# Spreading first in each slot, and one bank for the rows of both norms, in a convolution-attention and mixture-of-experts block

## The chip, the cores and the metric

One core of one Trainium2 chip. The metric is the device time of one execution in microseconds (us); the kernel before takes 705.34 us, the median of three runs (703.17 to 705.60).

## The reference

For x of shape (4, 64, 128, 128), fp32, per pixel (token) of 64 channels:

```python
n = ln_c(x)                                  # over channels, eps 1e-6
k, q, v = relu(Wk n + bk), relu(Wq n + bq), Wv n + bv      # 8 heads of 8 channels
context = einsum('bhkn,bhvn->bhkv', k, v)    # one sum over all 16384 pixels of an image
x = x + Wr einsum('bhkv,bhkn->bhvn', context, q) + br
t = tokens(x); m = ln_t(t)                   # over channels, eps 1e-5
p = softmax(m @ router_w + router_b)         # 8 experts, the two largest kept, scaled to sum 1
x = t + sum_over_two(p_e * (m @ expert_w[e] + expert_b[e]))
```

## The kernel before

The pixels are cut into 32 groups of 2048 (`GROUPS`, 8 for each image); a group is two halves of the image rows on partitions 0 to 63 and 64 to 127 (`S` = 2), in two halves of 512 columns (`U` = 2). The program is one long software pipeline of 49 steps (`STEPS`) of four slots each, and every engine walks through the same loop over steps `n` and slots `k`, written by hand. A stage with lag `L` works at step `n` on group `n - L`. In a step with all stages at work TensorE does, in order:

- slot 0: `make_keys` (L936, L943), `to_columns` twice (transposing the row statistics of both norms, L1006), `turn_x` (L911);
- slot 1: `sum_up` (the context's sums, L974), `turn_back` (L921);
- slot 2: `attend` (L1020), `make_queries` (L960);
- slot 3: `turn_gates` (L1045), `measure_x` and `route` (both through `rows_of`, L986: for each token the mean, the mean square and the router's products).

Each slot then ends with two pieces of the expert stage. `broadcast(i)` (the spreading, L1059) copies the gate of a pair of experts to 64 partitions per expert for the two iterations of the next slot; from its banks VectorE multiplies one half with x (`product`, L816, writes `z`) and ScalarE copies the other (`copy_gates`, L571, writes `gbs`) for GpSimd to multiply (L431). `experts(i)` (L1073, L1076, opened once per half group by the bias product L1070) multiplies `z` of this slot's two iterations with the expert weights, in an output bank of its own. There are 8 iterations per group, 2 per slot (`PER_SLOT`). `experts` with j = 0 waits until VectorE's `result` (L826) has taken the output bank of the half group before; `result` stands in slots 0 and 2.

All other products go through six banks in turn. `bank_uses` lists the uses in the program's order; a use waits until the use six places before it was taken out of its bank:

```python
USE = {use: (i % ROUND, i // ROUND + 1) for i, use in enumerate(bank_uses())}
```

VectorE's queue holds in each slot: fold, `result`, `add_sums` (L688), `x_deviations` (a chain of 7 small operations, L654 to L657 and L642 to L644), `residual` (L720), a piece of `gates` (27 operations for two groups, spread over 8 slots by `gates_by_phase`, with a square root and an exponential on ScalarE between them), `normalise` (L676), and last the two products of the slot. GpSimd does its products first in each slot and the squares of x (L422) in slot 1. ScalarE takes the other banks.

## Time and profile before

| | |
|---|---|
| median of 3 runs | 705.34 us |
| profiled execution | 708.03 us, its span 706.2 us |
| TensorE busy | 647.4 us, 92% |
| VectorE busy | 532.2 us, 75% |
| ScalarE busy | 428.5 us, 61% |
| GpSimd busy | 396.5 us, 56% |
| mean granted TensorE clock | 0.99 |

PE is TensorE, PEld its weight loads, DVE VectorE, ACT ScalarE, POOL GpSimd, SP the engine that issues most transfers. Busy times are unions over an engine's instructions, so the shares are averages over stretches of the pipeline in which different stages work: from step 0 to 16 no experts, from step 32 on no more loading of x. In a timeline a line is one instruction or a run of like ones; the ends of matmuls are modelled and overlap the next start, so distances are read from start to start. A matmul of fp32 shows as two passes.

### The profile page before, as it was taken

To read this page: it belongs to the slowest core of one execution; us is meant where nothing else is said; L and a number is where in the kernel's file an instruction comes from. 1 tells how busy PE (TensorE), PEld (TensorE's weight loads), DVE (VectorE), ACT (ScalarE), POOL (GpSimd) and SP (SyncE) were. 2 spreads that over 40 slices of the span, in tenths; PEclk is the share of its full clock that TensorE was granted. 3 is DMA by queue.
4 is the path that set the end of the run, shared out by engine and by line. 5 is a ranking of instruction groups with operands and counts; after the bars stand their busy time and mean duration, and the time that the engine had idled before them with its cause. 6 is when DMAs were issued, how large, how long until landed. Compare 5 with 4: busy or idle time off the path is not lost.

```text
span 706.2 us, 20616 instructions
## 1 busy us (share of the span) xinstructions
PE 647.4 (92%) x7846; PEld 302.0 (43%) x7846; DVE 532.2 (75%) x1176; ACT 428.5 (61%) x852; POOL 396.5 (56%) x350
## 2 busy tenths in 40 slices
PE   3898999799999999999999999999989889896786
PEld 1676766444544444444544444444322223231221
DVE  3443456878788988888788988867889998978853
ACT  2354556857566676657576776756656666564542
POOL 7132342165456566565456566555657667575785
PEclk9999999999999999999999999999999999999999
DMA  6232544655565555555566564444656555454442
GB/s 141 61 75 71 130 122 122 169 145 123 136 151 135 136 140 125 127 136 123 133 150 148 123 148 99 98 111 107 149 130 152 120 120 135 102 131 97 107 104 46
DMA packets 32660, 86.16 MB, mean 122 GB/s; under 512 B 7650, under 2 KB 7826, under 8 KB 32562
## 3 DMA queue, kind: packets, MB, share of 16 engines
q1 hardware_dynamic: 32082, 84.64, 50.7%
q8 instruction: 63, 1.03, 0.7%
q0 software_dynamic: 288, 0.19, 0.1%
q14 instruction: 35, 0.29, 0.1%
q10 hardware_dynamic: 192, 0.01, 0.0%
HBM read 34.47 MB, written 16.78 MB: 73 GB/s over the span
## 4 chain that ended last, share of the span: by engine, by line
PE 68%; DVE 13%; ACT 10%; issue 7%; DMA 1%; POOL 1%; DVEq 0%; SPq 0%; ACTq 0%; POOLq 0%
PE bank L1073 25%; PE bank L1059 8%; PE bank L986 5%; PE bank L921 5%; PE bank L974 5%; PE bank L943 4%; PE bank L911 4%; ACT grows L565 3%; DVE z L816 3%; PE bank L1020 3%; PE bank L1006 2%; ACT L543 2%; DVE osb L826 2%; PE bank L1070 2%; DVE x L720 2%
## 5 line engine op out<-in xcount | busy, mean ns | idle before, releaser
L431 POOL TENSOR_TENSOR z<-gbs,x1d 128x512 f32<-128x512 f32 x256 | 320.6, 1275 | 220.7 <-ACT gbs L571 164.8
L1076 PE MATMUL bank<-z,ew 128*64 128x512 f32 x512 | 248.0, 607 | 0.0
L1073 PE MATMUL bank<-z,ew 128*64 128x512 f32 x512 | 247.9, 607 | 0.0
L571 ACT COPY gbs<-bank 128x512 f32<-128x512 f32 x256 | 140.0, 593 | 95.3 <-PE bank L1059 94.4
L816 DVE TENSOR_TENSOR z<-bank,x1d 128x512 f32<-128x512 f32 x256 | 162.9, 677 | 20.4 <-PE bank L1059 20.1
L1059 PE MATMUL bank<-grows,sel 64*64 64x512 f16 x1024 | 89.3, 388 | 28.2 <-DVE z L816 17.0
L422 POOL TENSOR_TENSOR xsq<-xin 128x512 f32<-128x512 f32 x64 | 65.6, 1046 | 81.8 <-DMA xin<-in_x_dram 78.2
L1073 PEld LDWEIGHTS bank<-z,ew 128*64 128x64 f32 x512 | 65.7, 138 | 105.6 <-issue 95.8
L492 ACT COPY xn<-bank 128x512 f32<-128x512 f32 x64 | 34.6, 588 | 68.2 <-PE bank L921 68.2
L676 DVE TENSOR_TENSOR xnT<-bank,rstd 128x512 f32<-128x512 f32 x64 | 41.3, 684 | 39.2 <-PE bank L911 37.0
L1059 PEld LDWEIGHTS bank<-grows,sel 64*64 64x64 f16 x1024 | 24.1, 104 | 97.2 <-issue 34.4
L1076 PEld LDWEIGHTS bank<-z,ew 128*64 128x64 f32 x512 | 65.6, 138 | 0.0
L826 DVE TENSOR_TENSOR osb<-bank,x 128x512 f32<-128x512 f32 x64 | 43.8, 685 | 23.1 <-PE bank L1076 23.1
L565 ACT COPY grows<-bank 128x1024 f16<-128x1024 f16 x32 | 32.3, 1010 | 30.3 <-PE bank L1045 30.3
L474 ACT ACTIVATE keys<-bank 128x512 f32<-128x512 f32 x64 | 34.8, 595 | 25.4 <-PE bank L943 25.4
L720 DVE SCALAR_TENSOR_TENSOR x<-bank,br_col,x_again 128x512 f32<-128x512 f32 x64 | 44.9, 743 | 5.2 <-PE bank L1020 4.8
L482 ACT ACTIVATE q<-bank,bq_col 128x512 f32<-128x512 f32 x64 | 40.6, 689 | 7.2 <-PE bank L960 7.2
L974 PEld LDWEIGHTS bank<-xnT,keys 128*64 128x64 f32 x1024 | 34.7, 139 | 13.3 <-issue 12.2
L974 PE MATMUL bank<-xnT,keys 128*64 128x66 f32 x1024 | 36.7, 225 | 1.2 <-ACT keys L474 1.0
L921 PE MATMUL bank<-k,xnT 128*128 128x128 f32 x256 | 35.9, 284 | 1.7 <-DVE xnT L676 1.2
L532 ACT ACTIVATE x1sq<-x 128x512 f32<-128x512 f32 x64 | 37.4, 645 | 0.0
L943 PEld LDWEIGHTS bank<-wk_bd,xn 64*64 64x64 f32 x2048 | 35.5, 135 | 4.2 <-issue 1.9
(138 smaller groups left out, 885.0 us busy)
## 6 DMA issues: line engine op xcount, KB each, us to landing
x1d<-x SPq DMA_DIRECT2D x128, 256.0 KB, 4.5
xin<-in_x_dram SPq DMA_DIRECT2D x64, 256.0 KB, 4.1
x_again<-in_x_dram SPq DMA_DIRECT2D x64, 256.0 KB, 4.1
out_dram<-osb SPq DMA_DIRECT2D x128, 128.0 KB, 2.4
k<-in_const_dram SPq DMA_DIRECT2D x1, 453.5 KB, 3.7
ew_nat<-in_L_ffn_expert_w_dram POOLq DMA_DIRECT2D x2, 64.0 KB, 6.5
sel<-in_const_sel_dram SPq DMA_DIRECT2D x1, 128.0 KB, 3.5
bk_rows<-bk_wide ACTq DMA_DIRECT2D x6, 1.0 KB, 1.7
```

What stands on the lines that cost most here:

```text
L422: pool.tensor_tensor(xsq[:, u * NT:(u + 1) * NT], half, half, ALU.mult).then_inc(x_squared, 1)
L431: pool.tensor_tensor(z[:, 1, i % R_Z, :], gbs[:, i % R_Z, :], x1d[:, g % 2, 1, u * NT:(u + 1) * NT], ALU.mult).then_inc(z_pool, 1)
L571: nc.scalar.copy(gbs[:, i % R_Z, :], bank[:, :]).then_inc(taken_of(("spread", i, 1)), 1)
L720: dve.scalar_tensor_tensor(x1[:, g % R_X1, half], bank[:, :], br_col[:, 0:1], x_again[:, g % 2, half], ALU.add, ALU.add).then_inc(taken_of ...
L816: dve.tensor_tensor(z[:, 0, i % R_Z, :], bank[:, :], x1d[:, g % 2, 0, u * NT:(u + 1) * NT], ALU.mult).then_inc(taken_of(("spread", i, 0)), 1)
L826: dve.tensor_tensor(osb[:, g % 2, half], out_bank[:, :], x1[:, g % R_X1, half], ALU.add).then_inc(out_done, 1)
L921: ins = pe.transpose(bank[:, j * P:(j + 1) * P], xnT[:, g % 2, u, j, 1:P + 1], eye)
L943: ins = pe.matmul(banks[s][C * a:C * a + C, j * C:(j + 1) * C], xn[rows, g % 2, j * P + C * a:j * P + C * a + C], wk_bd[rows, rows], start ...
L974: ins = pe.matmul(bank[C * s:C * s + C, 0:C + 2], keys[:, s, at:at + C], xnT[:, g % 2, u, j, C * s:C * s + C + 2], start=(u == 0 and j == ...
L1059: ins = pe.matmul(bank[cols, :], sel[rows, j, cols], grows[rows, g % 2, u * NT:(u + 1) * NT], start=True, stop=True)
L1073: pe.matmul(out_bank[0:C, :], ew[:, j, :], z[:, 0, i % R_Z, :], start=False, stop=(j == PAIRS - 1), skip_group_check=True).then_inc(prod_d ...
L1076: pe.matmul(out_bank[C:P, :], ew[:, j, :], z[:, 1, i % R_Z, :], start=False, stop=(j == PAIRS - 1), skip_group_check=True).then_inc(prod_d ...
```

## The change

Four edits:

1. In each slot of each engine's loop the expert stage's parts that concern the next slot come first: `broadcast` on TensorE, `product` on VectorE, `copy_gates` on ScalarE. `experts` stays last. `x_deviations` moves behind the gates on VectorE, `root_x` from slot 1 to slot 2, `square_x1` ahead of the rows' eviction on ScalarE.
2. The row statistics of the norm of x (group n) and of the router (group n - 12) are accumulated in one bank, at other rows of it (`NROW` = 24 of each 32), taken with one eviction to `rows_sb`, and turned by one pair of transpositions instead of two; ScalarE takes two slices of that one bank, `lg` and `xs`.
3. `turn_gates` and the eviction of the gate rows move from slot 3 with lag 16 to slot 1 with lag 17. The experts' lag goes from 17 to 18, so that there are 50 steps. The ring of x1 has 8 places instead of 7.
4. The pieces of the gates chain are cut and placed anew.

```diff
-L_COLS, L_TURN, L_KEYS, L_AGAIN, L_ATTEND, L_ROUTE, L_GATES, L_TURN_GATES, L_EXPERTS = 1, 2, 3, 9, 11, 12, 14, 16, 17
+L_COLS, L_TURN, L_KEYS, L_AGAIN, L_ATTEND, L_ROUTE, L_GATES, L_TURN_GATES, L_EXPERTS = 1, 2, 3, 9, 11, 12, 14, 17, 18
-R_X, R_Q, R_X1, R_Z = 3, 8, 7, 4
+R_X, R_Q, R_X1, R_Z = 3, 8, 8, 4
...
-            p, late = divmod(SLOTS * (n - L_GATES) + k - 1 - phase, 2 * SLOTS)
+            p, late = divmod(SLOTS * (n - L_GATES) + k - 3 - phase, 2 * SLOTS)
...
-            gate_steps = {0: root_dev, 5: exponent, 7: high, 8: low}
+            gate_steps = {0: root_dev, 4: exponent, 7: high, 8: low}
...
-            gates_by_phase = {8: (26, 27), 0: (0, 4), 2: (4, 9), 3: (9, 12), 4: (12, 16), 6: (16, 20), 7: (20, 26)}
+            gates_by_phase = {8: (26, 27), 0: (0, 4), 1: (4, 8), 2: (8, 13), 4: (13, 16), 5: (16, 18), 6: (18, 24), 7: (24, 26)}
...
+            def take_cols(n):
+
+                bank = when_filled(act, ("cols", n, 0))
+                columns = bank[:, 0:U * P].rearrange("p (a r) -> p a r", r=W)
+                g = n - L_ROUTE
+                if real(g):
+                    upto(act, gate_dve, (g // 2 - 2) * N_GATE + 8)
+                    half = g % 2 * U * NJ
+                    ins = nc.scalar.copy(lg[:, g // 2 % 2, half:half + U * NJ, :], columns[:, :, 0:NLG])
+                if real(n):
+                    upto(act, xstat_dve, n * N_XSTAT)
+                    ins = nc.scalar.copy(xs[:, :, :], columns[:, :, NLG:NROW])
+                ins.then_inc(taken_of(("cols", n, 0)), 1)
...
+            def make_rows(n):
...
+                for part, (tile, weights) in enumerate(parts):
+                    chunks = tile.rearrange("p (u j n) -> p u j n", u=U, j=NJ)
                     for j in range(NJ):
-                        ins = pe.matmul(outs[j], weights, chunks[:, :, j, :], start=start, stop=not start,
-                                        skip_group_check=True)
+                        out_rows = bank[W * j:W * (j + 1), 0:U * P].rearrange("p (u n) -> p u n", u=U)
+                        ins = pe.matmul(out_rows, weights, chunks[:, :, j, :], start=(part == 0),
+                                        stop=(part == len(parts) - 1), skip_group_check=True)
...
                 for k in range(SLOTS):
+                    for i in iterations(n, k + 1):
+                        product(i)
+
                     if folding(n, k):
                         fold(*folding(n, k))
                     if k == 0 and real(n - L_EXPERTS - 1):
                         result(n - L_EXPERTS - 1, 1)
...
-                    for i in iterations(n, k + 1):
-                        product(i)
...
                 for k in range(SLOTS):
+                    for i in iterations(n, k + 1):
+                        broadcast(i)
+
                     if folding(n, k):
                         fold(*folding(n, k))
...
-                    for i in iterations(n, k + 1):
-                        broadcast(i)
                     for i in iterations(n, k):
                         experts(i)
```

TensorE's queue in slots 1 and 2 of a full step, before (L974 context sums, L921 turning back, L1059 spreading, L1073 and L1076 experts, L1020 attention, L960 queries, L1070 bias product):

```order
257 L974 MATMUL bank<-xnT,keys 64x66 x16
258 L921 MATMUL bank<-k,xnT 128x128 x8
259 L1059 MATMUL bank<-grows,sel 64x512 x8
260 L1073 MATMUL bank<-z,ew 64x512
...
264 L1020 MATMUL bank<-q,att 64x512 x4
265 L960 MATMUL bank<-xn,wq 64x512 x4
266 L1059 MATMUL bank<-grows,sel 64x512 x8
267 L1070 MATMUL bank<-grows,eb_rows 64x512 x2
268 L1073 MATMUL bank<-z,ew 64x512
```

The same place in the changed kernel, whose line numbers differ (L1045 is now the spreading, L960 the context sums, L907 turning back, L1031 the gates' turning, L1006 attention, L946 queries, L1056 the bias product, L1059 an expert product):

```order
262 L1045 MATMUL bank<-grows,sel 64x512 x8
263 L960 MATMUL bank<-xnT,keys 64x66 x16
264 L907 MATMUL bank<-k,xnT 128x128 x8
265 L1031 MATMUL bank<-eye,gT 128x128 x8
266 L1059 MATMUL bank<-z,ew 64x512
...
270 L1045 MATMUL bank<-grows,sel 64x512 x8
271 L1006 MATMUL bank<-q,att 64x512 x4
272 L946 MATMUL bank<-xn,wq 64x512 x4
273 L1056 MATMUL bank<-grows,eb_rows 64x512 x2
274 L1059 MATMUL bank<-z,ew 64x512
```

The spreading now stands between the experts of the slot before and the slot's other work, and the bias product behind that other work. VectorE's queue at the start of slot 1 and in slot 2 of a step, before (L688 add_sums, L654 to L657 the first half of x_deviations, L762 to L788 gates, L816 the products, L826 `result`, L720 residual):

```order
335 L688 TENSOR_TENSOR s_acc<-bank,s_acc 128x66
336 L654 SCALAR_TENSOR_TENSOR xstat<-xs 128x16
...
339 L657 RECIPROCAL xstat<-xstat 128x16
340 L762 TENSOR_REDUCE gstat<-bank 128x32
...
343 L762 TENSOR_REDUCE gstat<-bank 128x32
344 L816 TENSOR_TENSOR z<-bank,x1d 128x512 x2
345 L826 TENSOR_TENSOR osb<-bank,x 128x512
346 L720 SCALAR_TENSOR_TENSOR x<-bank,br_col,x_again 128x512 x2
347 L816 TENSOR_TENSOR z<-bank,x1d 128x512 x2
```

and in the changed kernel (L803 the products, L675 add_sums, L770 to L749 gates, L641 to L644 x_deviations, L813 `result`, L707 residual):

```order
325 L803 TENSOR_TENSOR z<-bank,x1d 128x512 x2
326 L675 TENSOR_TENSOR s_acc<-bank,s_acc 128x66
327 L770 TENSOR_TENSOR bank<-bank,rb_row 128x256
...
331 L749 TENSOR_REDUCE gstat<-bank 128x32
332 L641 SCALAR_TENSOR_TENSOR xstat<-xs 128x16
...
335 L644 RECIPROCAL xstat<-xstat 128x16
336 L803 TENSOR_TENSOR z<-bank,x1d 128x512 x2
337 L813 TENSOR_TENSOR osb<-bank,x 128x512
338 L707 SCALAR_TENSOR_TENSOR x<-bank,br_col,x_again 128x512 x2
```

The products of a slot have moved from its end to its start, so that in slots 0 and 2 `result` stands behind products whose spreading is issued in the same slot.

## Rows read from the trace of the kernel before

**Rows 1.** Stretch, its us, busy PE PEld DVE ACT POOL, clock, DMA share, GB/s

```profile
0.00:143.41 143.41, 122.66 (x2226) 82.48 (x2226) 72.32 (x232) 76.55 (x173) 47.33 (x65) 0.99 0.47 113
143.41:440.38 296.97, 292.90 (x3674) 140.19 (x3674) 247.56 (x539) 197.96 (x398) 180.38 (x151) 1.00 0.56 133
440.38:497.32 56.94, 54.31 (x672) 24.89 (x670) 44.32 (x96) 38.36 (x73) 30.34 (x26) 1.00 0.48 115
497.32:634.25 136.93, 122.16 (x913) 38.06 (x913) 120.34 (x227) 83.80 (x155) 89.95 (x72) 0.98 0.54 126
634.25:706.20 71.95, 55.33 (x368) 16.39 (x366) 47.65 (x83) 31.85 (x56) 48.49 (x40) 0.97 0.40 92
```

**Rows 2.** Timeline, TensorE, a full step: start, us, line, [idle before <-releaser]

```profile
301.67 0.41 PE L936 MATMUL bank<-bk_rows,ones 64*64 64x512 bf16 x4
...
303.22 0.38 PE L1006 MATMUL bank<-k,route_rows 128*128 128x128 f32 x2
303.43 1.04 PE L911 MATMUL bank<-k,xin 128*128 128x128 f32 x8
304.40 0.63 PE L1059 MATMUL bank<-grows,sel 64*64 64x512 f16 x8
...
311.39 1.09 PE L1020 MATMUL bank<-q,att 64*64 64x512 f32 x8
...
313.16 0.60 PE L1059 MATMUL bank<-grows,sel 64*64 64x512 f16 x6
313.98 0.40 PE L1059 MATMUL bank<-grows,sel 64*64 64x512 f16 x2 [0.22 <-DVE x L720]
...
318.24 0.61 PE L986 MATMUL bank<-x1sq,k 128*32 128x256 f32 x8
318.95 0.63 PE L1059 MATMUL bank<-grows,sel 64*64 64x512 f16 x8
...
321.37 0.41 PE L936 MATMUL bank<-bk_rows,ones 64*64 64x512 bf16 x4
```

**Rows 3.** The same, TensorE, in step 47

```profile
684.86 0.63 PE L1059 MATMUL bank<-grows,sel 64*64 64x512 f16 x8
685.75 0.41 PE L1070 MATMUL bank<-grows,eb_rows 128*64 128x512 f16 x2 [0.26 <-DVE osb L826]
...
687.80 0.62 PE L1045 MATMUL bank<-eye,gT 128*128 128x128 f16 x8
689.53 0.63 PE L1059 MATMUL bank<-grows,sel 64*64 64x512 f16 x8 [1.10 <-ACT grows L565]
```

**Rows 4.** The same, VectorE, in step 47

```profile
685.00 0.69 DVE L826 TENSOR_TENSOR osb<-bank,x 128x512 f32<-128x512 f32 x1 [0.83 <-PE bank L1076]
...
690.03 1.29 DVE L816 TENSOR_TENSOR z<-bank,x1d 128x512 f32<-128x512 f32 x2 [3.14 <-PE bank L1059]
```

**Rows 5.** Groups by line: count, busy us, mean ns, idle before

```profile
L422 POOL TENSOR_TENSOR xsq<-xin 128x512 f32<-128x512 f32 x64 | 65.6, 1046 | 81.8 <-DMA xin<-in_x_dram 78.2 <-PE bank L986 3.6
...
L768 DVE TENSOR_TENSOR bank<-bank,gstat 128x256 f32<-128x256 f32 x32 | 13.8, 432 | 11.6 <-ACT gex L543 11.0
```

**Rows 6.** Timeline, GpSimd, step 47

```profile
690.73 4.97 POOL L431 TENSOR_TENSOR z<-gbs,x1d 128x512 f32<-128x512 f32 x4 [2.17 <-issue]
```

**Rows 7.** The same, GpSimd and VectorE, in step 36

```profile
516.75 2.50 POOL L431 TENSOR_TENSOR z<-gbs,x1d 128x512 f32<-128x512 f32 x2 [1.81 <-ACT gbs L571]
...
518.11 1.19 DVE L777 TENSOR_TENSOR bstat<-bstat,lg 128x32 f32<-128x32 f32 x1
```

**Rows 8.** The same, TensorE, keys' first product of steps 13, 16 and 17

```profile
102.38 0.41 PE L936 MATMUL bank<-bk_rows,ones 64*64 64x512 bf16 x4
...
128.12 0.41 PE L936 MATMUL bank<-bk_rows,ones 64*64 64x512 bf16 x4
...
143.41 0.41 PE L936 MATMUL bank<-bk_rows,ones 64*64 64x512 bf16 x4 [1.31 <-issue]
```

**Rows 9.** The same, TensorE, step 36

```profile
522.12 1.06 PE L1073 MATMUL bank<-z,ew 128*64 128x512 f32 x1
```

## What it does to the time: the prediction

> **What bounds the kernel now.** I read the busy table by stretches first, then TensorE's timeline in a full step, in the filling steps and in the tail, then what VectorE and GpSimd do beside it. The table by stretches [rows 1] is cut where the pipeline changes: filling (steps 0 to 16), full (17 to 31, 297.0 us), thinning (32 to 34), tail with gates, attention and experts (35 to 43, 136.9 us), and the last experts (44 to 48, 72.0 us). In the full stretch TensorE is busy 292.9 of 297.0 us: it is the bound, at 2.4 GHz, and VectorE follows with 247.6. In the tail TensorE has 122.2 of 136.9, in the last stretch 55.3 of 72.0; there waits decide.
>
> A full step takes 19.70 us (301.67 to 321.37) [rows 2]. Its TensorE waits are small: 0.22 us in slot 2, where the last spreading waits for a bank that VectorE's residual holds, and in slot 3 about 0.2 us, since the squares' products that started at 318.24 would be through by 318.75 and the spreading waits for the gate rows that ScalarE has just copied. The second transposition takes 0.21 us (303.22 to 303.43) [rows 2]. So what the change can win in a full step is: 0.2 transposition, 0.2 and 0.2 waits, one change of tile shape fewer (the first copy of an array shape takes 0.5 where a repeated one takes 0.4; I count 0.15 for the change), 0.25 for spreading beside keys and queries, which have its shape. Together 1.0: TensorE's own work becomes 18.7 us (slots of 5.06, 4.99, 4.36 and 4.28).
>
> **What the new order makes wait.** The bias product of a half group opens the output bank again, so it needs `result`, VectorE's eviction of the half before. Before, VectorE did `result` at once in slots 0 and 2. Now it does the two products of the slot first, and these need the spreading that TensorE issues at the slot's start. From the tail: spreading at 689.53, products from 690.03 when VectorE is idle (0.50; I take 0.47), the next instruction 1.20 after the first product's start (two take 1.29, ends overlap), `result` 0.69 [rows 3, 4], bias product 0.06 after it (osb from 685.00 + 0.69, bias 685.75) [rows 3, 4]. So the bias product can't start before 0.47 + 1.20 + 0.69 + 0.06 = 2.42 us into slots 0 and 2. Before it was 685.75 - 684.86 = 0.89 [rows 3]. What TensorE has in between hides it or not:
> - Slot 0 of a full step: spreading 0.48, then 304.40 - 301.67 - 0.21 = 2.52: 3.00 us [rows 2]. Hidden if VectorE is less than 0.6 late.
> - Slot 2: 0.48 + (313.16 - 311.39) + 0.1 = 2.33 us [rows 2]. No slack at all: any lateness of VectorE is TensorE idle time.
> - Slots 0 and 2 in the tail: 0.9 to 1.4 us, and at the end 0.56: 1.0 to 1.9 us of idle time each.
>
> **Is VectorE late in slot 2?** In slot 1 it now has two products (to 1.67), add_sums (to about 2.0), then five or six gate steps of 0.43 + 0.03 each (to 4.0 to 4.2) [rows 5] and the first four steps of x_deviations. GpSimd's products start 1.20 us after the spreading (690.73 against 689.53) and take 1.24 each [rows 3, 6]; with the two squares behind them at 1.02 each [rows 5] it is busy from 1.2 to 5.7 us of the slot. A small VectorE operation that starts beside one of GpSimd's takes as long as what is left of it: 1.19 us at 518.11 for 128x32 elements, ending at 519.30, 0.05 after GpSimd's second product (516.75 + 2.50) [rows 7]. Before, the four steps of x_deviations ran while GpSimd was idle; now two of them (in even steps a gate step too) fall beside its squares. I get VectorE free 6.3 us after slot 1's start, slot 2 starting at 5.0 and its products wanted at 5.5: 0.4 to 0.9 late, so 0.4 to 1.0 idle on TensorE in slot 2. In odd steps the square root and `low` on ScalarE stand ahead of slot 0's copies, the three Newton steps of the gates fall beside GpSimd's products, `normalise` ends at about 5.8 to 6.2 and sum_up waits up to 0.6 for its bank. Both kinds of step come to 18.7 + 0.95 = **19.65 us**: the win is given back.
> The Trainium skill (SBUF - State Buffer, Who interferes with whom) says that a VectorE instruction with two SBUF inputs, or in a two-port mode, shares a port pair with GpSimd as an exclusive lock. By that the held ones are the same as in the rows, so its sum is mine; it also lets VectorE hold GpSimd, for which the rows give no size.
>
> **The extra step.** Gate copies and turning move to slot 1 of a step later, so experts start in step 18 and there are 50 steps, not 49. Evictions of rows and columns on ScalarE (0.39 and less) lie beside other work; the x1 ring of 8 and the DMA queue's order change no wait that I see: the spread x1 of a group is still asked for more than a step ahead.
>
> **The sum**, in us of the profiled span:
> - Filling: steps 13 to 15 take 8.58 each (102.38 to 128.12) and step 16 takes 15.29, with VectorE's first gates in it [rows 8]. Those three lose 0.21 each. Steps 16 and 17 now share the gate work that crowded step 16: VectorE some 11 and 10.8, TensorE 8.4 and 9.5. 102.38 + 25.1 + 21.8 = 149.3; 143.4 before: +5.9.
> - Full: 14 x 19.65 + 1.5 (folding, 297.0 - 15 x 19.70) = 276.6: -20.4.
> - Thinning: the full step less the x rows (0.87), then also GpSimd's squares and less lateness, then also turning and back (2.0): 18.8 + 18.1 + 16.4 = 53.3: -3.6.
> - Tail, nine steps: slots 4.48 (2.42 + bias 0.24 + experts 1.82), 2.98, 4.48, 3.4 = 15.3, plus VectorE's lateness, 0.5 in slot 2 and 1.0 in every other slot 0: 16.4. 147.6: +10.7.
> - The last: three steps of 15.9 with gates left, two of 4.48 + 2.98 + 4.48 + 2.43 = 14.35, and 17.4 with the store (2.43 is the spreading's 0.56 + (687.80 - 685.75 - 0.24) + 0.05 [rows 3]): 93.8 against 72.0: +21.8. The 1.10 us that spreading waited for the gate rows goes here [rows 3], but 2 x 1.53 more wait for `result` come.
> - Clock: in the tail of before it was at 1.2 GHz for some stretches (an expert product takes 1.06 us at 522.12, where it takes 0.59 at full clock) [rows 9], 1.5 us each time, three times. TensorE was then idle for 1.5 us and shorter pieces. Idle stretches of 1.9 to 2.9 us twice a step are longer: as many drops or more; +3. The ends are no drop beyond those three, 0, and one more in each of ten steps, +15.
> Total 5.9 - 20.4 - 3.6 + 10.7 + 21.8 + 3 = +17.4. The profiled execution took 708.03 (span 706.2), the median is 705.34; taken from the median: 722.7, said as **722 us**.
>
> **Rivals.**
> - VectorE is not late (15%). The held operations fall into GpSimd's gaps, for instance since its products start later. Decides below 0.1 us of lateness in slot 2. Then the full step is 18.7 and the tail step 15.85: 149.3 + 263.3 + 52 + 142.7 + 91.1 = 698.4, -7.8: **697.5 us**, faster. For it: my slot schedule is made of 0.2 us pieces; against it: VectorE has 247.6 us of work in 297.0 already [rows 1], before more of it is held.
> - Only the tail pays (15%): full steps at 18.9, tail as forecast: 149.3 + 266.1 + 52 + 147.6 + 93.8 = 708.8, +2.6: **708 us**, about no change.
> - The clock halves in most tail steps (15%): ten drops of 1.5 more: **736 us**. For it: TensorE's share goes from 89% to about 83% in the tail and from 77% to about 60% at the end, and before the mean clock is 0.98 and 0.97 there against 1.00 in the full stretch [rows 1]. Against: 0.98 also says that most of the tail's waits cost no clock. The Trainium skill (TensorE: Matmul & The Clock Gate, HAM oscillation) has the clock fall to half where TensorE idles between bursts, and advises against such gaps; that rule speaks against this change and is this rival's mechanism.
> - The merging does less than it says: the order shows one pair of transpositions where two were, so only its size (0.2 a step, in 20 steps, 4 us) can be off; inside the range.
>
> **Chances.** Forecast 55%, the rivals 15% each. A difference under 0.5% (3.5 us) can't be told from no change. Faster: the first rival and a bit of the second, 17%; the same: 13%; slower: 70%. Range: 700 to 738; the first rival's centre and the worst of the clock are left out, together under 2 in 10.
>
> **What would show it.** Right: 50 steps, the first expert product near 152 us; full steps of 19.4 to 19.9 us with TensorE waiting 0.4 to 1 us ahead of the bias product in slot 2, released by `result`; in the last steps 4.4 to 4.5 us for slots 0 and 2 with 1.8 us of idle time there; no wait for the gate rows; mean of VectorE's small operations in slot 1 raised. Wrong: full steps at or below 18.9 us, or bias products released by anything else. Then the lateness of VectorE was mis-sized.

## The result and the profile after

The changed kernel takes **739.4 us** (median of four runs, 737.7 to 740.9) against 705.5 for the kernel before on the same chip: a ratio of 1.048, 95% interval 1.043 to 1.053. It is slower, as forecast, but by 33.9 us where 17.4 were forecast; the range ended at 738.

The busy table by stretches, cut as in [rows 1] (filling to the first step with experts, full, thinning, tail, last experts; columns: us, busy PE PEld DVE ACT POOL, clock, DMA share, GB/s):

```profile
0.00:153.08 153.08, 130.95 (x2384) 87.87 (x2384) 79.43 (x247) 79.90 (x178) 49.46 (x67) 0.98 0.45 109
153.08:435.07 281.99, 270.14 (x3406) 125.18 (x3402) 247.11 (x510) 182.51 (x361) 170.17 (x142) 1.00 0.56 132
435.07:489.97 54.90, 52.94 (x668) 23.72 (x666) 45.21 (x92) 37.19 (x72) 30.12 (x24) 1.00 0.50 116
489.97:643.21 153.24, 123.39 (x916) 38.01 (x914) 124.69 (x231) 83.55 (x157) 90.11 (x72) 0.96 0.51 119
643.21:739.10 95.89, 68.55 (x444) 19.51 (x442) 53.55 (x97) 37.22 (x67) 57.35 (x47) 0.95 0.35 80
```

Against [rows 1]: filling +9.7, full -15.0 (one step fewer in it), thinning -2.0, tail +16.3, last +23.9 us. TensorE was the bound in the full stretch of before; now it is idle for 12 of 282 us there and for 30 of 153 in the tail. Most of TensorE's waiting has one releaser, `result` (osb) (us in total, times, longest):

```profile
PE bank L1056 <- DVE osb L813: 53.3, 31, 3.1
PE bank L982 <- POOL xsq L421: 11.1, 2, 9.9
PE bank L992 <- ACT rows_sb L496: 4.5, 7, 1.9
PE bank L946 <- DVE z L803: 3.7, 9, 0.5
PE bank L960 <- ACT keys L473: 2.8, 2, 1.5
```

All 31 waits for osb come after the full stretch; the first is at 474.90. In full steps the bias product doesn't wait. There the products of slot 2 are late (266.94 where the spreading at 265.88 would allow about 266.35), and TensorE waits one instruction earlier: the queries need the bank that the second product takes. The waits of 0.2 us or more in a pair of full steps are these (a step with the longer and one with the shorter wait):

```profile
247.64 1.09 PE L946 MATMUL bank<-xn,wq 64*64 64x512 f32 x8 [0.53 <-DVE z L803]
248.84 0.41 PE L1056 MATMUL bank<-grows,eb_rows 128*64 128x512 f16 x2
...
257.55 1.09 PE L897 MATMUL bank<-k,xin 128*128 128x128 f32 x8 [0.23 <-ACT gbs L562]
261.46 1.15 PE L960 MATMUL bank<-xnT,keys 128*64 128x66 f32 x32 [0.20 <-DVE xnT L663]
267.63 1.09 PE L946 MATMUL bank<-xn,wq 64*64 64x512 f32 x8 [0.26 <-DVE z L803]
```

The last steps show the forecast wait in its pure form. TensorE in step 48 (spreading, bias product, spreading of the next slot), where [rows 3] has 0.26 us in the bias product's place:

```profile
707.57 0.63 PE L1045 MATMUL bank<-grows,sel 64*64 64x512 f16 x8
709.95 0.41 PE L1056 MATMUL bank<-grows,eb_rows 128*64 128x512 f16 x2 [1.76 <-DVE osb L813]
712.01 0.63 PE L1045 MATMUL bank<-grows,sel 64*64 64x512 f16 x8
```

709.95 - 707.57 = 2.38 us into the slot (forecast 2.42), the slot 4.44 (forecast 4.48), idle 1.76 (forecast 1.8). In a tail step with gates it is worse. VectorE in slots 3 and 0 of steps 38 and 39:

```profile
552.33 1.29 DVE L803 TENSOR_TENSOR z<-bank,x1d 128x512 f32<-128x512 f32 x2 [0.49 <-PE bank L1045]
553.54 0.69 DVE L736 TENSOR_TENSOR bank<-bank,gT 128x512 f32<-128x512 f32 x1
554.13 0.77 DVE L721 SCALAR_TENSOR_TENSOR bstat<-lg 128x32 f32<-128x32 f32 x1
554.94 1.20 DVE L764 TENSOR_TENSOR bstat<-bstat,lg 128x32 f32<-128x32 f32 x1
556.17 0.18 DVE L765 TENSOR_SCALAR bstat<-bstat 128x32 f32<-128x32 f32 x1
556.39 0.35 DVE L766 RECIPROCAL bstat<-bstat 128x32 f32<-128x32 f32 x1
556.66 1.22 DVE L803 TENSOR_TENSOR z<-bank,x1d 128x512 f32<-128x512 f32 x2
557.80 0.68 DVE L813 TENSOR_TENSOR osb<-bank,x 128x512 f32<-128x512 f32 x1
```

and GpSimd and TensorE beside it:

```profile
553.57 2.52 POOL L430 TENSOR_TENSOR z<-gbs,x1d 128x512 f32<-128x512 f32 x2 [3.04 <-ACT gbs L562]
```

```profile
555.25 0.63 PE L1045 MATMUL bank<-grows,sel 64*64 64x512 f16 x8
555.81 0.44 PE L992 MATMUL bank<-k,rows_sb 128*128 128x128 f32 x2
558.53 0.64 PE L1056 MATMUL bank<-grows,eb_rows 128*64 128x512 f16 x2 [2.29 <-DVE osb L813]
558.96 1.06 PE L1059 MATMUL bank<-z,ew 128*64 128x512 f32 x1
```

The first gate operation ends with GpSimd's first product and the second, of the same 128x32 elements, with GpSimd's second (553.57 + 2.52 = 556.09; 554.94 + 1.20 = 556.14). A third, behind them, takes 0.18. So the products start at 556.66 and not at 555.7, `result` at 557.80, and TensorE, idle for 2.29 us, comes back at half clock: an expert product takes 1.06 us where it takes 0.59. That happens in seven places of the tail and the last steps, four and three (before: two and one, one of them [rows 9]), each time behind a wait of 2.17 to 3.07 us for osb. A wait of such a length doesn't always do it: behind one of 2.28 us at 525.76 the clock stayed at full speed.

To compare kernels of different lag I cut all their spans by one mark, the start of the bias product of a group: filling up to group 0, full from there to group 15, tail to group 27, last to the end of the span. The labels are those of the experiments below; all in us, from one profiled execution of each. With a lag of 18 "full" holds one thinner step, so kernels of equal lag compare best.

| kernel | filling | full | tail | last |
|---|---|---|---|---|
| before | 146.7 | 297.0 | 191.5 | 71.0 |
| after | 158.1 | 299.3 | 206.0 | 75.8 |
| e1_result_first | 158.0 | 305.1 | 189.1 | 64.4 |
| e2_merge_only | 142.5 | 294.6 | 189.9 | 73.5 |
| e3_old_order | 159.9 | 304.9 | 174.7 | 61.2 |
| e7_no_holds | 156.9 | 290.7 | 172.4 | 60.7 |
| e7b_old_no_holds | 157.1 | 308.1 | 173.0 | 60.8 |
| e7c_after_no_holds | 158.0 | 285.5 | 194.7 | 74.7 |
| e13_lag18 | 154.1 | 292.4 | 187.4 | 59.2 |
| e12_phases | 140.4 | 293.3 | 186.2 | 68.6 |
| e15_phases_split | 142.0 | 293.3 | 175.5 | 66.2 |

### The profile page after: what moved, and what is told of

It reads as the page before. It is cut to its first block, busy times and chain, and to the rows that moved or that the text cites. A ratio compares the mean times of both kernels' runs of the same rounds, so it can differ in the third digit from the quotient of the medians.

```text
span 739.1 us, 20475 instructions
## 1 busy us (share of the span) xinstructions
PE 646.0 (87%) x7806; PEld 294.3 (40%) x7806; DVE 550.0 (74%) x1176; ACT 420.4 (57%) x832; POOL 397.2 (54%) x350
## 4 chain that ended last, share of the span: by engine, by line
PE 57%; DVE 28%; issue 10%; ACT 3%; DMA 1%; POOL 1%; DVEq 0%; SPq 0%; ACTq 0%; POOLq 0%
PE bank L1059 22%; DVE z L803 8%; PE bank L982 6%; PE bank L1045 5%; PE bank L897 4%; DVE osb L813 4%; PE bank L960 3%; PE bank L1056 3%; PE bank L907 3%; PE bank L929 2%; PE bank L946 2%; DVE bstat L764 2%; DVE gstat L749 2%; PE bank L1006 1%; PE bank L992 1%
## 5 line engine op out<-in xcount | busy, mean ns | idle before, releaser
L430 POOL TENSOR_TENSOR z<-gbs,x1d 128x512 f32<-128x512 f32 x256 | 320.7, 1275 | 244.3 <-ACT gbs L562 244.3
L1059 PE MATMUL bank<-z,ew 128*64 128x512 f32 x512 | 252.9, 618 | 0.0
L1062 PE MATMUL bank<-z,ew 128*64 128x512 f32 x512 | 252.9, 618 | 0.0
L803 DVE TENSOR_TENSOR z<-bank,x1d 128x512 f32<-128x512 f32 x256 | 162.9, 678 | 94.5 <-PE bank L1045 94.3
L562 ACT COPY gbs<-bank 128x512 f32<-128x512 f32 x256 | 137.7, 592 | 158.9 <-PE bank L1045 158.8
L1059 PEld LDWEIGHTS bank<-z,ew 128*64 128x64 f32 x512 | 66.3, 139 | 99.0 <-issue 78.9
L1045 PE MATMUL bank<-grows,sel 64*64 64x512 f16 x1024 | 82.1, 395 | 0.2 <-DVE x L707 0.2
L1056 PE MATMUL bank<-grows,eb_rows 128*64 128x512 f16 x128 | 26.5, 411 | 54.6 <-DVE osb L813 53.3
L1045 PEld LDWEIGHTS bank<-grows,sel 64*64 64x64 f16 x1024 | 18.8, 105 | 109.0 <-issue 90.1
L707 DVE SCALAR_TENSOR_TENSOR x<-bank,br_col,x_again 128x512 f32<-128x512 f32 x64 | 44.7, 739 | 5.4 <-PE bank L1006 5.4
L523 ACT ACTIVATE x1sq<-x 128x512 f32<-128x512 f32 x64 | 37.0, 628 | 17.3 <-PE bank L982 17.1
L813 DVE TENSOR_TENSOR osb<-bank,x 128x512 f32<-128x512 f32 x64 | 43.5, 679 | 4.0 <-PE bank L1062 4.0
L960 PE MATMUL bank<-xnT,keys 128*64 128x66 f32 x1024 | 38.0, 227 | 4.5 <-ACT keys L473 2.8
L1056 PEld LDWEIGHTS bank<-grows,eb_rows 128*64 128x64 bf16 x128 | 7.0, 106 | 87.5 <-DVE osb L813 84.8
L960 PEld LDWEIGHTS bank<-xnT,keys 128*64 128x64 f32 x1024 | 33.6, 140 | 14.2 <-issue 9.7
L946 PE MATMUL bank<-xn,wq 64*64 64x512 f32 x256 | 34.3, 605 | 3.8 <-DVE z L803 3.7
```

What stands on the lines that cost most here:

```text
L430: pool.tensor_tensor(z[:, 1, i % R_Z, :], gbs[:, i % R_Z, :], x1d[:, g % 2, 1, u * NT:(u + 1) * NT], ALU.mult).then_inc(z_pool, 1)
L562: nc.scalar.copy(gbs[:, i % R_Z, :], bank[:, :]).then_inc(taken_of(("spread", i, 1)), 1)
L707: dve.scalar_tensor_tensor(x1[:, g % R_X1, half], bank[:, :], br_col[:, 0:1], x_again[:, g % 2, half], ALU.add, ALU.add).then_inc(taken_of ...
L803: dve.tensor_tensor(z[:, 0, i % R_Z, :], bank[:, :], x1d[:, g % 2, 0, u * NT:(u + 1) * NT], ALU.mult).then_inc(taken_of(("spread", i, 0)), 1)
L813: dve.tensor_tensor(osb[:, g % 2, half], out_bank[:, :], x1[:, g % R_X1, half], ALU.add).then_inc(out_done, 1)
L946: ins = pe.matmul(banks[s][cols, :], wq_4[rows, cols], xn[rows, g % 2, u * NT:(u + 1) * NT], start=True, stop=True)
```

## Experiments

### Where `result` stands, and the parts of the change by themselves

**e1_result_first**

```diff
+ if k == 0 and real(n - L_EXPERTS - 1):
+     result(n - L_EXPERTS - 1, 1)
+ if k == 2 and real(n - L_EXPERTS):
+     result(n - L_EXPERTS, 0)
  for i in iterations(n, k + 1):
      product(i)
...
- if k == 0 and real(n - L_EXPERTS - 1):
-     result(n - L_EXPERTS - 1, 1)
...
```

> The changed kernel with one edit: on VectorE `result` stands ahead of the two products in slots 0 and 2, products stay ahead of everything else. Theory 1 (the output bank is freed late because `result` queues behind two products that themselves wait for TensorE's spreading): the 31 waits of the bias product for osb (53.3 us together) go; some of that comes back as other waits, so 35 to 50 us less: 689 to 704 us; last steps 12.3 to 13 us instead of 14.28, tail steps 13 to 14.5 instead of 15.8 and 17, full steps 19.2 to 19.6 instead of 19.83. Rival (VectorE is late by itself, from small operations held beside GpSimd, and `result` would be late at the head of the slot too): at most 15 us less, 724 us or more, and the bias product still waits 1 us or more for osb.

719.3 us, ratio to before 1.021 (1.016 to 1.025): 20 less than the changed kernel, between the two expectations. The last two steps take 11.28 us, better than forecast, but full steps rise to 20.1 and tail steps still take 14.7 and 15.9. TensorE's waits:

```profile
PE bank L1056 <- DVE osb L813: 21.9, 22, 2.4
PE bank L946 <- DVE z L803: 11.6, 12, 1.1
PE bank L992 <- ACT rows_sb L496: 7.3, 11, 1.9
```

In full steps the products, now behind `result`, take their banks' contents later and the queries wait for the bank (L946). In the tail `result`, first in its slot, is still late. VectorE and GpSimd in such a slot:

```profile
649.21 0.63 DVE L721 SCALAR_TENSOR_TENSOR bstat<-lg 128x32 f32<-128x32 f32 x1
649.87 1.18 DVE L764 TENSOR_TENSOR bstat<-bstat,lg 128x32 f32<-128x32 f32 x1
651.09 0.18 DVE L765 TENSOR_SCALAR bstat<-bstat 128x32 f32<-128x32 f32 x1
651.31 0.35 DVE L766 RECIPROCAL bstat<-bstat 128x32 f32<-128x32 f32 x1
651.58 0.63 DVE L813 TENSOR_TENSOR osb<-bank,x 128x512 f32<-128x512 f32 x1
```

```profile
648.52 2.49 POOL L430 TENSOR_TENSOR z<-gbs,x1d 128x512 f32<-128x512 f32 x2 [1.73 <-ACT gbs L562]
```

Again the held operation ends with GpSimd (651.01).

**e2_merge_only**: before, with `rows`, `cols`, make_rows and take_cols of the change, nothing moved otherwise (take_rows where take_stat_rows stood).

> The kernel before with only the merging: rows of both norms in one bank, one eviction ahead of the gate copies in slot 3, one transposition, one bank of columns; order of the slots and lag of 17 as before. Theory: 0.2 us of TensorE less in each of 20 steps with both norms and nothing else, 700 to 705 us. Rival (the one eviction now waits for the x1 rows too, and gate copies stand behind it): 707 to 715 us.

701.5 us, 0.994 (0.992 to 0.997). The merging gives its 0.16 us in each full step (19.38 and 19.54 for 19.54 and 19.70) and 4 us in all, give or take 2. The forecast had 4 from 0.2 us in each of 20 steps; that the total agrees is partly luck, since the stages give 4.2 in the filling, 2.4 in the full stretch and 1.6 in the tail, and lose 2.5 in the last steps.

**e3_old_order**

```diff
- for i in iterations(n, k + 1):
-     broadcast(i)
  if folding(n, k):
      fold(*folding(n, k))
...
+ for i in iterations(n, k + 1):
+     broadcast(i)
  for i in iterations(n, k):
      experts(i)
```

and the same for product, copy_gates and the uses of banks; x_deviations and take_rows back in their places.

> The changed kernel with spreading, products and gate copies put back at the slot's end (and take_rows and x_deviations where they stood), keeping the merging, the lag of 18 (50 steps) and the new gate schedule. Theory 1 (the new order is what costs): 700 to 710 us, the extra step costing about 3 (one filling step of 8.6 and one tail step of 13.5 more, one full step of 19.7 less, with the merging's 4 less). Rival (the extra step, the new gate phases or the merging cost it): 722 us or more.

698.7 us, 0.991 (0.989 to 0.994): faster than before and **40.6 us** faster than the changed kernel, which differs from it by the order alone (that of `x_deviations` and take_rows included). By the stages the new order loses 31.3 us in the tail and 14.6 in the last steps, and gains 1.9 in the filling and 5.6 in the full stretch (38.4 of span).

**e4_squares_slot0**

```diff
- if k == 1 and real(n):
+ if k == 0 and real(n):
      for u in range(U):
          square_x(n, u)
```

> The changed kernel with one edit: GpSimd's two squares of x go from slot 1 to slot 0, so x_deviations' first four steps in slot 1 stand beside no square. Theory 2 (held small operations make VectorE late in slot 2): VectorE's busy time falls by 5 to 10 us, full steps get 0.2 to 0.4 us shorter, nothing changes behind the last x (tail and last steps), so 733 to 736 us. Theory 1 alone: 738 to 741 us. If the squares now hold normalise or the gates in slot 0 instead, 740 to 745.

741.2 us, 1.052 (1.047 to 1.057): nothing. x_deviations is held no more (445 to 203 ns for its first step), but gate operations of slot 0 now are. Full steps alternate 19.17 and 20.69 where they alternated 19.68 and 19.98: the held time moved to the neighbour. So which operations are held can be chosen by a slot, but this choice hardly lowers the sum: VectorE's busy time goes from 550.0 to 548.2 us.

### Taking the holds away

**e5_rows_first**

```diff
+ if has_rows(n):
+     take_rows(n)
  if real(n - L_ATTEND):
      for u in range(U):
          square_x1(n - L_ATTEND, u)
- if has_rows(n):
-     take_rows(n)
```

> The changed kernel with one edit: on ScalarE take_rows stands ahead of the two squares of x1 in slot 3. Theory 3 (the rows are evicted about 1 us late, so the transposition of slot 0 waits for rows_sb in the filling steps and the keys' banks come late): the waits of L992 for rows_sb (4.5 us in 7) go and those of L960 for keys (2.8) shrink, 3 to 5 us less: 734 to 736 us, all of it before the first expert product. Rival (the squares of x1 then come late instead, and make_rows of the next step with them, or nothing moves): 738 to 741 us.

737.6 us, 1.047 (1.043 to 1.050), 1.8 less than the changed kernel and inside what two kernels' medians scatter by. In the trace the waits for rows_sb fall from 4.5 to 1.4 us and those for the keys' eviction grow from 2.8 to 4.7; the first bias product comes 1.3 us earlier, nothing else changes. The mechanism is there, but its size is 1 to 2 us, not 3 to 5.

**e7_no_holds**

```diff
- lambda: dve.scalar_tensor_tensor(work[0], root, -0.5, root, ALU.mult, ALU.mult),
- lambda: dve.tensor_tensor(work[1], work[0], variance, ALU.mult),
- lambda: dve.scalar_tensor_tensor(out, work[1], 1.5, root, ALU.add, ALU.mult)
+ lambda: dve.reciprocal(work[0], root),
+ lambda: dve.reciprocal(work[1], work[0]),
+ lambda: dve.reciprocal(out, work[1])
...
```

> The first experiment's kernel (`result` first), with VectorE's ten small operations on two inputs from SBUF, or on one with two constants (in newton, x_deviations and gates), replaced by reciprocals of the same size, of which no trace shows one held by GpSimd (353 and 253 ns in every kernel). This leaves the deviations of both norms out of the computation. The six kinds on bstat and gstat took 70 us in the first experiment and take 34 as reciprocals. Theory 2 (what stands in the way of `result` is gate work that GpSimd holds): the remaining 22 waits for osb (21.9 us) halve, the tail's steps get 1 us shorter each, full steps 0.2 to 0.4: 700 to 709 us. Rival (the number and place of the gate steps decides, not the holds): 713 to 719 us.

This kernel and the two that follow leave the deviations of both norms and an addition in the gates out, so what they write is not the block's result; they serve for timing only. 683.5 us, 0.971 (0.968 to 0.975): **35.8 us** less than e1_result_first, where I expected 10 to 19. VectorE's busy time falls by 33.7 us (555.8 to 522.1), and the five drops of the clock in e1_result_first's tail and last steps are gone. Full steps are 18.97 and 19.02 (20.1 before), tail steps 13.9 and 14.1 (14.7 and 15.9). The reciprocals take the same time wherever they stand; `scale` (L741), which I left alone, is held still:

```profile
L741 DVE TENSOR_TENSOR bank<-lg,bstat 128x256 f32<-128x256 f32 x16 | 12.1, 755 | 0.6
...
L630 DVE RECIPROCAL bstat<-bstat 128x32 f32<-128x32 f32 x16 | 5.7, 353 | 0.5
```

beside the same line of the changed kernel:

```profile
L630 DVE TENSOR_TENSOR bstat<-bstat 128x32 f32<-128x32 f32 x16 | 17.4, 1085 | 0.6
```

**e7c_after_no_holds** and **e7b_old_no_holds** put the same reciprocals into the changed kernel and into e3_old_order.

> The changed kernel itself (`result` behind the products) with the same reciprocals; the deviations are left out. Theory 1 and 2 as two separate costs: `result` behind the products still costs the 28 us in tail and last steps less 6 in the full ones that the first experiment showed, so 683.5 + 20 = 700 to 708 us, with the last steps at 14.28 again. Rival (one cause: without holds VectorE catches up and the place of `result` matters little): 684 to 692 us. Rival (holds matter only where `result` is first): 725 or more.

716.1 us, 1.015 (1.012 to 1.018): 23.3 less than the changed kernel (VectorE's busy time 24.4 less, 550.0 to 525.6) and 32.6 more than e7_no_holds. So there are two separate costs, and that of `result` is larger than I had put it (716.1 where I expected 700 to 708). In its regular full steps the profile lists no wait of TensorE: they take 18.70 and 18.86 us, which is the 18.7 that the prediction had counted as TensorE's own work. The tail keeps the wait for `result`: halves of 7.82 to 8.09 us, last steps 14.28.

```profile
PE bank L1056 <- DVE osb L813: 49.4, 31, 2.4
```

> The old-order kernel (merging, lag 18, new gate schedule, order of before) with the same reciprocals in place of VectorE's held small operations; the deviations of both norms are left out here too. It took 698.7 us with them. Theory 2 in its strong form (the holds are what the new order loses by; the old order has them where they cost little): 687 to 697 us, so slower than the 683.5 of the new order without holds. Rival (holds cost every order about as much, 34 us with `result` first): 662 to 672 us.

700.6 us, 0.993 (0.991 to 0.995), 2 more than with the operations. Both sides of the expectation were off, the second by nearly 30 us. But this run takes hardly anything away: a reciprocal of 353 ns is longer than an operation that isn't held (0.18), and the old order holds its small operations much less. VectorE's busy time falls by 2.1 us only (519.6 to 517.5). The group that took 1085 ns in the changed kernel takes 257 in e3_old_order, where its line is L629:

```profile
L629 DVE TENSOR_TENSOR bstat<-bstat 128x32 f32<-128x32 f32 x16 | 4.1, 257 | 0.6
```

Taking the means of all these small operations (on bstat, gstat, xstat) above 175 or 180 ns, what they take when not held, the held time comes to about 67 us in the changed kernel, 70 in e1_result_first, 36 in e3_old_order and 45 in the kernel before; the reciprocals add about 32 us in each. That is an estimate from the `--lines` means. With the new order the time falls by about what VectorE's busy time falls by (23.3 for 24.4, 35.8 for 33.7); with the old one neither moves by more than about 2.

The six kernels together, in us:

| order | with holds | without |
|---|---|---|
| new, `result` behind the products (the change) | 739.4 | 716.1 |
| new, `result` first | 719.3 | 683.5 |
| old | 698.7 | 700.6 |

**e11_result_first_split** and **e10_old_split** keep the whole computation and shorten the holds:

```diff
- pool.tensor_tensor(z[:, 1, i % R_Z, :], gbs[:, i % R_Z, :], x1d[:, g % 2, 1, u * NT:(u + 1) * NT],
-                    ALU.mult).then_inc(z_pool, 1)
+ for c in range(0, NT, NT // 2):
+     ins = pool.tensor_tensor(z[:, 1, i % R_Z, c:c + NT // 2], gbs[:, i % R_Z, c:c + NT // 2],
+                              x1d[:, g % 2, 1, u * NT + c:u * NT + c + NT // 2], ALU.mult)
+ ins.then_inc(z_pool, 1)
```

> The first experiment's kernel (719.3 us) with each of GpSimd's products cut into two of 256 columns, all of the computation kept. Theory 2: holds are halved, which gives back half of the 36 us that taking them away gave: 699 to 708 us. Rival (it was not the holds but the reciprocals' data or their timing): 716 us or more.

706.3 us, 1.000 (0.998 to 1.003): 13 less than without the split, a third of what taking the holds away gave. Its values are those of the unsplit kernel, so at least this third has nothing to do with values; that e7b_old_no_holds, with the values of e7_no_holds, is no faster than e3_old_order speaks against them for the rest.

> The old-order kernel with each of GpSimd's products cut into two of 256 columns. If a held operation of VectorE waits for the end of one GpSimd instruction, the longest hold is halved (from 1.2 to about 0.65 us), and VectorE's small operations take 10 to 15 us less in all; GpSimd pays a fixed price for 256 more instructions, perhaps 0.1 us each, half a us per slot of four, and has room for it. 692 to 698 us. Rival (the price of the halves puts the products' end on the path, or GpSimd gets held by VectorE more): 699 to 706 us.

698.3 us, 0.990 (0.987 to 0.994): no change, though VectorE's busy time falls by 8.1 us (519.6 to 511.5). This is the better test of holds in the old order: there a few us of them cost nothing. A half takes 731 ns, so two cost 187 more than the one of 1275, and last steps go from 11.28 to 11.74 us, four slots of four halves each: 16 halves of 731 ns make 11.70, so there GpSimd is the bound.

```profile
L431 POOL TENSOR_TENSOR z<-gbs,x1d 128x256 f32<-128x256 f32 x512 | 356.9, 731 | 172.5 <-ACT gbs L564 158.5 <-issue 11.3 <-PE bank L1064 2.6
```

### Where the gate steps stand, and the lag

**e9_gates_02**, on e1_result_first:

```diff
- gates_by_phase = {8: (26, 27), 0: (0, 4), 1: (4, 8), 2: (8, 13), 4: (13, 16), 5: (16, 18), 6: (18, 24), 7: (24, 26)}
+ gates_by_phase = {8: (26, 27), 0: (0, 4), 1: (4, 9), 3: (9, 13), 4: (13, 16), 5: (16, 20), 7: (20, 26)}
```

> The first experiment's kernel, with the gate steps of slot 1 (five or six of them, ahead of `result` in slot 2) moved into slots 0 and 2, behind the products; slot 3 as before. Theory 4 (in the new order gate steps stand between a slot's products and the next `result`, which has no slack, since TensorE opens the output bank again within 0.5 us of the slot's start; in the old order they stand between `result` and products that are wanted a slot later): waits for osb in slot 2 go, tail steps fall from 15.3 to 14 or less, full steps may rise by 0.2: 703 to 712 us. Rival (any place of the same work gives the same lateness): 716 to 720 us.

724.9 us, 1.029 (1.025 to 1.032), slower than its parent by 5.6. Waits for osb do fall (21.9 to 15.1 us), the last steps gain 0.6 us, but waits for products (L992 and L1045 for z: 15.6 us) and for rows_sb (10.8) come in their place and the full stretch rises from 305.1 to 308.7. So gate steps delay whatever stands behind them wherever they go. But the edit is no clean test of their place: VectorE's busy time rises from 555.8 to 582.5 us, since in slots 0 and 2 more of them are held, and that alone could make the 5.6 us.

**e8_merge_rows_slot2**: e2_merge_only, with turn_gates and take_gate_rows in slot 2.

> The merging-only kernel with one more edit: the gate rows are turned and copied in slot 2 of step n - 16 and not in slot 3, where the spreading waits for them; lag 17, old order. Theory: the wait of about 1.1 us at each of the last steps and 0.2 us in the full ones goes, last steps 11.3 us instead of 12.46, full steps 19.2 to 19.4 instead of 19.46, tail steps with both (16.97) a little shorter: 689 to 697 us. Rival (low is late on ScalarE in slot 1 and attend and queries now stand behind that wait): 701 to 708 us.

723.5 us, 1.027 (1.024 to 1.030), the rival and worse: the turning waits for `low` on ScalarE, 37 us in 16 waits.

```profile
PE bank L1033 <- ACT gT L550: 37.0, 16, 3.4
```

So with this gate schedule the gate rows can't be turned a slot earlier; experts that come later are the other way to make room.

**e13_lag18**: e2_merge_only with `L_EXPERTS = 18`, an x1 ring of 8 and gate rows in a ring of three.

> The merging-only kernel with the experts one step later (lag 18, 50 steps; gate rows still turned in slot 3 of step n - 16, in a ring of three, so that nothing waits for them), gate steps as before. Theory 6 (lag and gate schedule are two things; the late filling comes from the step more, and the loss in full steps from the new gate schedule): first bias product 8.6 to 10 us later than in merging-only (151 to 153 us), full steps 19.2 to 19.5 us, last steps 11.3 instead of 12.46: 695 to 701 us. Rival (the lag itself makes full steps 19.9 us): 703 to 710 us.

694.9 us, 0.988 (0.982 to 0.994). Against e2_merge_only the lag puts 11.6 us into the filling (more than the 8.6 of one plain step; the added step has gates in it, which may be why) and leaves full steps at 19.38. So the 19.94 of e3_old_order come from the new gate schedule with the turning in slot 1 (the two weren't separated), as does its shorter tail (174.7 for 187.4).

**e12_phases**: e2_merge_only with

```diff
- gates_by_phase = {8: (26, 27), 0: (0, 4), 2: (4, 9), 3: (9, 12), 4: (12, 16), 6: (16, 20), 7: (20, 26)}
+ gates_by_phase = {8: (26, 27), 0: (0, 4), 2: (4, 9), 3: (9, 12), 4: (12, 16), 5: (16, 18), 6: (18, 22), 7: (22, 26)}
```

and the exponent one slot earlier.

> The merging-only kernel (lag 17, old order, 701.5 us) with VectorE's gate steps spread more: two of the four of slot 3 go to slot 2 and two of the six of slot 0 to slot 3, the exponent one slot earlier. Theory 5 (in the tail's even steps of 16.97 us the spreading waits 1.4 us twice for a bank whose product stands behind six and five gate steps): 2 to 3 waits less in six such steps, 6 to 10 us less, full steps 0 to 0.3 longer: 693 to 701 us. Rival (the held steps of slot 1 decide, and more gate steps beside the residual in slot 2 cost the full steps): 702 to 708 us.

690.4 us, 0.980 (0.974 to 0.986): 11 less, at no cost in the full steps (19.38). The even steps of 17 us stay, though; what goes is the crowding in the filling (2.1), outliers behind them (steps of 18.64 to 15.48 and 20.77 to 17.13) and 4.9 in the last stage, which holds the second of these. The expected size came from another place than the expected one.

**e14_merge_split**: e2_merge_only with the halves.

> The merging-only kernel with each of GpSimd's products cut into two of 256 columns. Theory 2: in the tail's slots 0 and 1 three operations held for 1.15 to 1.19 us each take about 0.65, so the even steps go from 16.97 to about 15.8; full steps unchanged; 694 to 698 us. Rival (as in the old order with lag 18, where the split gave nothing): 700 to 703 us.

693.1 us, 0.985 (0.981 to 0.988): as expected, tail's even steps from 16.97 to 15.82, full steps unchanged.

**e15_phases_split** and **e16_phases_lag18**:

> The merging-only kernel with both the spread gate steps (alone 690.4 us) and GpSimd's products in halves (alone 693.1 us). If they act on different waits: tail's even steps from 17.1 to about 15, 683 to 687 us. If both shorten the same wait: 689 to 691 us.

**678.7 us**, 0.961 (0.958 to 0.964), the fastest kernel here: the even tail steps fall to 14.13, further than the two edits alone let expect. I read that as two parts of one chain (products behind gate steps behind a hold) whose end decides; it wasn't tried by itself. The clock helps too: there are no drops in this kernel, three in e2_merge_only. Full steps stay at 19.38. Its stages full, tail and last:

```profile
142.02:435.36 293.34, 290.00 (x3646) 137.98 (x3644) 245.51 (x544) 194.47 (x382) 196.90 (x270) 1.00 0.56 135
435.36:610.85 175.49, 170.06 (x1507) 60.25 (x1503) 154.62 (x319) 122.41 (x224) 132.66 (x192) 1.00 0.56 133
610.85:677.00 66.15, 53.37 (x360) 16.58 (x356) 43.38 (x80) 31.57 (x55) 53.04 (x77) 1.00 0.42 99
```

> The merging-only kernel with the spread gate steps and the lag of 18 (alone 694.9 us). If the lag's gain is that nothing waits for gate rows in the last steps and slot 3, it comes on top: 683 to 688 us. If it is the gate steps' place again: 689 to 694 us.

684.1 us, 0.968 (0.964 to 0.972): the lag's 6 us come on top. Lag and split together weren't tried.

## Why the prediction was right and where it was wrong

**The direction was right, and so was the mechanism of the tail and the last steps.** The named wait, `result` behind two products that wait for the slot's own spreading, is the changed kernel's largest (53.3 us in 31), its place and size in the last steps are met to 0.05 us, and putting `result` first takes 20 us off. TensorE's own work of 18.7 us a full step is what e7c_after_no_holds runs at, though no run separates the 0.15 us that the forecast counted for the tile shapes. Also met: no wait for gate rows, more drops of the clock, and, partly by luck, the merging's 4 us.

**In the full stretch the wait stood elsewhere.** The prediction had TensorE wait 0.4 to 1 us ahead of the bias product in slot 2, released by `result`. It never does so in a full step. VectorE is late, as forecast (0.6 us in slot 2 of the step shown), but TensorE meets this one instruction earlier, at the queries, which wait 0.53 and 0.26 us for a bank that the second product takes, and there are shorter waits ahead of `turn_x` (0.23) and of the sums (0.20). The cost, put at 0.95 us a full step, is 19.83 - 18.78 = 1.05: the size is met, the place is not. The waits of 0.2 us or more that the profile lists make 0.6 of it; where the rest lies is open.

**What was mis-sized**, term by term against the profiled span (forecast, measured):

| term | forecast | measured | missing |
|---|---|---|---|
| filling | +5.9 | +9.7 | 3.8 |
| full | -20.4 | -15.0 | 5.4 |
| thinning | -3.6 | -2.0 | 1.6 |
| tail | +10.7 | +16.3 | 5.6 |
| last | +21.8 | +23.9 | 2.1 |
| clock, put apart | +3 | in the stretches | -3.0 |

The sum is 15.5 short. Every stage cost more than forecast; the steps that failed are the terms below, the tail and the full stretch above all.

*Filling.* The step that failed is "Steps 16 and 17 now share the gate work that crowded step 16". They took 153.08 - 126.74 = 26.3 us, not 21.8, step 17 alone 16.0. I had counted VectorE and TensorE in it, not ScalarE's order: at its head `high`'s casts and the squares of x1 stand ahead of take_rows, then the root and `low` ahead of the keys' eviction.

```profile
140.37 0.41 PE L992 MATMUL bank<-k,rows_sb 128*128 128x128 f32 x2 [1.90 <-ACT rows_sb L496]
140.61 1.04 PE L897 MATMUL bank<-k,xin 128*128 128x128 f32 x8
142.99 2.03 PE L960 MATMUL bank<-xnT,keys 128*64 128x66 f32 x32 [1.34 <-ACT keys L473]
144.94 1.97 PE L907 MATMUL bank<-k,xnT 128*128 128x128 f32 x8
```

```profile
137.84 1.07 ACT L543 CAST gT<-bank 128x256 f16<-128x256 f32 x2 [0.68 <-DVE bank L786]
138.80 1.16 ACT L523 ACTIVATE x1sq<-x 128x512 f32<-128x512 f32 x2
139.85 0.37 ACT L496 COPY rows_sb<-bank 128x256 f32<-128x256 f32 x1
...
140.80 1.07 ACT L549 ACTIVATE gT<-bank 128x256 f16<-128x256 f32 x2
141.76 1.09 ACT L473 ACTIVATE keys<-bank 128x512 f32<-128x512 f32 x2
```

Behind these waits TensorE ran at half clock for some 5 us (eight transpositions 1.97 us, 1.04 a moment earlier). The sentence "Evictions of rows and columns on ScalarE (0.39 and less) lie beside other work" was wrong there. Putting take_rows first gave back 1.3 us of it.

*Full.* 14 steps of 19.83 for 19.65 make 2.5 us; the rest is "1.5 (folding)", where 4.4 were measured. That term was misread in the first place: before, full steps take 19.70 and 19.54 in turn, so each of the two foldings costs 20.34 + 20.21 - 19.70 - 19.54 = 1.3 us, 2.6 in all. In the changed kernel the second (314.83 to 355.72, two steps) costs 1.2, no more than before; the two steps of the first (153.08 to 195.84) take 3.1 more than regular ones. So 1.9 us belong not to folding but to the first steps with experts, where the keys start after 1.08 us of idle time and `turn_x` waits 0.54.

*Tail.* "plus VectorE's lateness, 0.5 in slot 2 and 1.0 in every other slot 0" and "+3" for the clock. Without holds the tail steps are 15.8, where the forecast's base was 15.3: slot 2 takes 4.85 and 5.11 in turn and not 4.48 us, since the five gate steps of slot 1, held or not, end 0.4 us after the products could start (e7c_after_no_holds: spreading 578.74, products 579.61). With holds and drops they are 17.0 on average. The clock fell in four places of the tail and three of the last steps, two more than before in each, at 1.7 us each (a slot of 5.33 us took 7.01). The third rival had ten more drops: the right thing, too many. The Trainium skill (TensorE: Matmul & The Clock Gate, HAM oscillation) warns of idle gaps between bursts; the trace agrees in that all seven drops stand behind a wait of 2.17 us or more, but no length of one wait decides by itself (below).

**What the forecast laid to the wrong part.** It gave the tail's and the last steps' loss to the new order and the extra step at once. Taken one after the other, the merging gives 4.0 us, the lag 6.6, the new gate schedule with turning in slot 1 takes 3.9, and the order takes 40.6: together the 33.9 measured. The first three are small beside their intervals (2 us either way for the merging, 4 for the other two), so that the gate schedule costs anything is not shown by the medians. The order's price was thus more than twice the 17.4 forecast, and part of it was paid back by the lag, which I had priced as a cost. Half of the order's price is `result` (20.1 us; without holds the same move gives 32.6, so the shares depend on which is taken away first). The other half, 719.3 - 698.7 = 20.6, is what GpSimd holds with `result` first (35.8), less what the new order wins by itself (700.6 - 683.5 = 17.1), and 1.9 that the reciprocals cost the old order. I had priced the holds' effect in full steps, to 0.1 us, and did not see that with `result` first they decide whether the order is worth having. The new order also makes more of them: about 67 us of held time where the old one has 36.

**Rivals.** "VectorE is not late" is the kernel without holds: its full step of 18.7 is right, its total of 697.5 isn't (716.1, the filling and the slots with gates being longer), and as shown VectorE was late. "Only the tail pays" falls with full steps of 19.83. "The merging does less" falls with e2_merge_only.

**Still open**: what holding costs the old order. It has about half as much of it, and the split took 8 us off VectorE there for nothing; that the held operations stand ahead of products wanted a slot later would explain this, but wasn't tried by itself. Why the two new orders gained about as much time as VectorE lost busy time is open as well; the extra 4 us of the filling beyond ScalarE's waits are not split between clock and waits.

## What to carry to other kernels

Before putting work first in every slot, ask of each in-order engine what it is put ahead of, and when TensorE reopens that bank: an eviction that TensorE wants at the head of the next slot has no slack, while products for the next slot have a whole one. Test a change of several parts by its parts and by undoing its order alone: here three parts were worth some 7 us of gain together, and the fourth lost 41. And where GpSimd streams in long instructions beside short work of VectorE, make its instructions shorter, or the short ones such that they aren't held, before reordering anything: spreading gate steps and halving GpSimd's products took the old order from 701.5 to 678.7 us.

## What the runs showed of the hardware

- A short VectorE operation on two SBUF operands that meets a running GpSimd instruction ends with that instruction, up to 1.25 us for one that takes 0.18 to 0.19. In the changed kernel's timeline 87 of 90 such small operations of over 0.3 us end with one of GpSimd's, and none of the short ones lies inside one. That was seen for 128x16, 128x32 and 128x256 elements. A tensor_scalar with one input can be held as well (520 ns on average at L783, 193 in e4_squares_slot0); a reciprocal of the same operands never was, in any kernel here (253 and 353 ns), nor the products that read one operand from PSUM (675 to 683 ns). The Trainium skill (SBUF — State Buffer, Who interferes with whom) says that an instruction with at most one SBUF input and outside the two-port modes doesn't contend, and that tensor_scalar can enter such a mode: the trace agrees.
- Held time counts as busy time, and in the new orders it was paid about in full: replacing the held operations took 24.4 and 33.7 us off VectorE's busy time and 23.3 and 35.8 off the kernels with the new order. With the old order, 8.1 us of busy time less (e10_old_split) gave nothing.
- A GpSimd product of 256 columns takes 731 ns and one of 512 1275: by these two sizes some 187 ns are fixed (an estimate, 2 x 731 - 1275).
- TensorE's clock fell from 2.4 to 1.2 GHz behind waits of 1.48 to 3.07 us, but the length of the last wait doesn't tell when. All seven drops in tail and last steps of the changed kernel, and both of e7c_after_no_holds, stand behind a wait of 2.17 to 3.07 us; yet behind waits of 2.28 us at 525.76 in the first and 2.36 us at 638.23 in the second there is none. In the kernel before two of the three drops stand behind 1.48 us (with one of 1.40 us 4.8 us earlier), while the same pair at 547.36 and 552.14 cost no clock; in e1_result_first four stand behind 1.49 to 1.53. With 2.28 us at 524.12, e5_rows_first has a drop in the very step where the changed kernel has none. After the wait of 2.29 us three products took 1.06 us each.
